# Edge weights of attention and convolution as two 128-row products over 448 columns instead of four 64-row products over 224

## The reference, cut to what matters

```
x = _layernorm(x + L0(x, edge_attr_16, edge_attr_4, ...))   # attention over edges
x = _layernorm(x + L1(x, edge_attr_64, edge_attr_4, ...))   # convolution over edges

L0:  w1 = rbf @ W_rbf                 # rbf (E,16), W_rbf (16,224): five sets of edge weights
     m1_s, m1_v = _cg_tp(msg_s, msg_v, y0, y1, w1[:, :64], w1[:, 64:128],
                         w1[:, 128:160], w1[:, 160:192], w1[:, 192:224])
L1:  w  = edge_query @ tp_weight      # edge_query (E,64), tp_weight (64,224)
     # the same five kinds of products of node features, edge directions and w,
     # then a sum over the edges of each target node
```

## Time and profile before

| | us |
|---|---|
| median of 3 runs | 7921.6 |
| lowest and highest | 7917.41, 7922.39 |
| the profiled execution, its own time | 7914.6 |
| its span | 7912.8 |

### The profile page before, as it was taken

The page is one execution under the profiler, slowest core; times in us unless marked ns, Lnnn a source line. Parts: engine busy times, 40 slices in busy tenths (PEclk is TensorE's granted clock), DMA queues, the critical chain, the costliest instruction groups (busy, mean ns, idle before and its releaser), DMA issues. The chain is left out here.

```text
span 7912.8 us, 199441 instructions
## 1 busy us (share of the span) xinstructions
PE 7045.1 (89%) x48227; PEld 5905.9 (75%) x48227; DVE 7568.2 (96%) x18615; ACT 5259.2 (66%) x18286; POOL 5348.1 (68%) x5500
## 2 busy tenths in 40 slices
PE   6999999999999999999999859998888888888888
PEld 4888888888888888888888848875555555555556
DVE  4999999999999999999999889976999999999999
ACT  2666666666666666666666634435788788788786
POOL 2777777777777777777777436634777777777773
PEclk5999999999999999999999979977999999999999
DMA  3444444434434344343434337732333333333332
GB/s 105 107 109 109 106 107 106 107 106 106 107 105 107 106 107 106 106 108 105 107 106 107 89 128 260 257 117 69 94 93 91 90 91 90 91 91 90 91 91 59
DMA packets 815660, 856.41 MB, mean 108 GB/s; under 512 B 413920, under 2 KB 623200, under 8 KB 815072
## 3 DMA queue, kind: packets, MB, share of 16 engines
q0 software_dynamic: 241920, 413.20, 21.8%
q1 hardware_dynamic: 573088, 438.30, 18.1%
q10 hardware_dynamic: 576, 4.01, 0.1%
HBM read 706.51 MB, written 148.44 MB: 108 GB/s over the span
## 5 line engine op out<-in xcount | busy, mean ns | idle before, releaser
L1243 POOL DMA_INDIRECT agg<-tab_conv,ce_idx x1808 | 1708.7, 945 | 841.3 <-issue 621.8
L471 POOL DMA_INDIRECT ae_gdst<-tab_dst,ae_idx x1616 | 1683.9, 1042 | 528.0 <-issue 528.0
L468 POOL DMA_INDIRECT ae_gsrc<-tab_src,ae_idx x1616 | 1538.5, 952 | 674.4 <-issue 523.9
L1333 PE MATMUL psum<-ce_prod,ce_plain 128*128 128x384 f32 x3616 | 1539.7, 507 | 302.5 <-ACT ce_prod L1318 302.1
L1318 ACT ACTIVATE ce_prod<-ce_raw,ce_y 128x64 f32<-128x64 f32 x5424 | 1464.8, 333 | 0.0
L1316 ACT ACTIVATE ce_prod<-ce_raw,ce_y 128x160 f32<-128x160 f32 x1808 | 753.2, 417 | 488.8 <-DVE ce_raw L1264 488.8
L1335 PEld LDWEIGHTS psum<-ce_prod,ce_plain 128*128 128x128 f32 x3616 | 687.6, 190 | 479.6 <-issue 1.5
L713 ACT ACTIVATE ae_second_t<-psum 128x512 f32<-128x512 f32 x1212 | 732.2, 604 | 462.0 <-PE psum L623 456.1
L1333 PEld LDWEIGHTS psum<-ce_prod,ce_plain 128*128 128x128 f32 x3616 | 546.9, 191 | 449.5 <-DVE ce_plain L1294 276.2
L631 PE MATMUL psum<-pack_sb,ae_first_t 128*128 128x200 f32 x3232 | 850.1, 345 | 2.2 <-ACT ae_first_t L709 2.0
L641 PE MATMUL psum<-pack_sb,ae_second_t 128*128 128x96 f32 x3232 | 665.1, 288 | 129.1 <-ACT ae_second_t L713 126.7
(11 more groups left out here) (216 smaller groups left out, 19066.1 us busy)
## 6 DMA issues: line engine op xcount, KB each, us to landing
ag_val<-h_dram SPq DMA_DIRECT2D x452, 320.0 KB, 4.0
h_dram<-ae_hout SPq DMA_DIRECT2D x404, 320.0 KB
agg<-in_query SPq DMA_DIRECT2D x452, 128.0 KB
ae_rin<-in_rin SPq DMA_DIRECT2D x404, 128.0 KB
agg<-tab_conv,ce_idx POOLq DMA_INDIRECT x1808
ae_gsrc<-tab_src,ae_idx POOLq DMA_INDIRECT x1616
ae_gdst<-tab_dst,ae_idx POOLq DMA_INDIRECT x1616
ce_idx<-in_eidx SPq DMA_DIRECT2D x452, 4.0 KB
```

Source lines behind the costliest of these rows:

```text
L468: pool.indirect_dma_start(gsrc[t.slot4][:, k, :], None, g["tab_src"], bass.IndirectOffsetOnAxis(ap=idx[t.slot4][:, k:k + 1], axis=0))\
L471: pool.indirect_dma_start(gdst[t.slot4][:, k, :], None, g["tab_dst"], bass.IndirectOffsetOnAxis(ap=idx[t.slot4][:, 4 + k:5 + k], axis=0))\
L1243: pool.indirect_dma_start(node[t.slot8][:, k, :], None, g["tab_conv"], bass.IndirectOffsetOnAxis(ap=idx[t.slot8][:, k:k + 1], axis=0))\
L1333: pe.matmul(b_a[t.slot], plain[t.slot4][:, k, :], prod[t.slot][:, k, 96:480], start=(k == 0), stop=False, skip_group_check=True)
```

## The change

The edge weights of both stages are made by two products over all 128 rows, each with 448 moving columns (224 for each of two edge tiles), one PSUM bank to a product. The weight matrices are laid out as blocks with zeros beside them so that the tiles stay apart: `wy` gets 4 x 224 columns, `tp` 448. The query values are laid out on the host so that rows 0 to 63 hold tile 0 (or 2) and rows 64 to 127 tile 1 (or 3). Three more constants are scaled at line 316, and a small tile of the softmax stage (`rows`) is placed in memory that `agg` leaves free there.

```diff
-    ("iota", 128, 128), ("wy", 128, 2 * WY), ...
+    ("iota", 128, 128), ("wy", 128, 4 * WY), ...
-    ("ts1", 64, 128), ("tv1", 96, 192), ("tp", 128, 224),
+    ("ts1", 64, 128), ("tv1", 96, 192), ("tp", 128, 448),
@@ attention_input
-                            for lo, hi, const in ((128, 160, 2 ** -0.5), (160, 192, 0.5), (192, 224, 3 ** -0.5)):
+                            for lo, hi, const in ((128, 160, 2 ** -0.5), (160, 192, 0.5), (192, 224, 3 ** -0.5),
+                                                  (352, 384, 2 ** -0.5), (384, 416, 0.5), (416, 448, 3 ** -0.5)):
@@ attention_edges, TensorE
-                        for k in (0, 2, 1, 3):
-                            q, half = slice(64 * (k // 2), 64 * (k // 2) + 64), WY * (k % 2)
-                            ins = pe.matmul(b_w[:, k, :], rbfy[t.slot][q, :], w("wy")[q, half:half + WY], start=True, stop=True)
+                        for k in (0, 2):
+                            ins = pe.matmul(b_w[:, k:k + 2, :], rbfy[t.slot][:, :], w("wy")[:, WY * k:WY * k + 2 * WY]
+                                            .rearrange("p (k c) -> p k c", k=2), start=True, stop=True)
@@ segment_softmax
-        rows = sb("rows", [H, 2, 2, P])
+        rows = g["agg"][0:H, :, :].rearrange("p b c -> p (b c)")[:, 0:4 * P].rearrange("p (d a q) -> p d a q", d=2, a=2)
@@ conv_edges, TensorE
-                        for k in (0, 2, 1, 3):
-                            q, e = CS * (k // 2), P * (k % 2)
-                            ins = pe.matmul(b_w[t.slot][:, k, :], query[t.slot8][q:q + CS, e:e + P], w("tp")[q:q + CS, :],
-                                            start=True, stop=True)
+                        for e in range(2):
+                            ins = pe.matmul(b_w[t.slot][:, 2 * e:2 * e + 2, :], query[t.slot8][:, P * e:P * e + P],
+                                            w("tp").rearrange("p (k c) -> p k c", k=2), start=True, stop=True)
@@ lay_pack, lay_inputs (host)
-    for lo in (0, 32, 64, 96):
-        own = W["wy"][lo:lo + 32, WY * (lo // 32 % 2):]
+    for k in range(4):
+        own = W["wy"][32 * k:32 * k + 32, WY * k:WY * k + WY]
-    W["tp"][0:64], W["tp"][64:128] = tp, tp
+    W["tp"][0:64, 0:224], W["tp"][64:128, 224:448] = tp, tp
-    query = np.pad(...).reshape(SUPER, 2, 256, 64)
-    query = query.transpose(0, 1, 3, 2).reshape(SUPER, P, 256)
+    query = np.pad(...).reshape(SUPER, 2, 2, P, 64)
+    query = query.transpose(0, 2, 4, 1, 3).reshape(SUPER, P, 256)
```

More of the change, by code:

```diff
@@ L49 @@
     ("ones", 128, 128), ("count", 128, STEPS), ("sidx", 128, 4),
-    ("iota", 128, 128), ("wy", 128, 2 * WY), ("m1_0", 128, 200), ("m1_1", 128, 96), ("m1_2", 96, 96), ("val_t", 64, 128),
+    ("iota", 128, 128), ("wy", 128, 4 * WY), ("m1_0", 128, 200), ("m1_1", 128, 96), ("m1_2", 96, 96), ("val_t", 64, 128),
     ("wg", 64, 32), ("adot", 128, 72), ("m2_0", 128, 96), ("m2_1", 128, 96), ("m2_2", 128, 96),
@@ L1545, in lay_inputs @@
     right = np.concatenate([y0, np.ones_like(rbf)], 2).reshape(SUPER, P, P)
-    query = np.pad(np.asarray(i["edge_attr_64"]), ((0, E - EDGES), (0, 0))).reshape(SUPER, 2, 256, 64)
-    query = query.transpose(0, 1, 3, 2).reshape(SUPER, P, 256)
+    query = np.pad(np.asarray(i["edge_attr_64"]), ((0, E - EDGES), (0, 0))).reshape(SUPER, 2, 2, P, 64)
+    query = query.transpose(0, 2, 4, 1, 3).reshape(SUPER, P, 256)
     return dict(
```

## The result

| | before | after |
|---|---|---|
| median | 7919.51 us (4 runs, 7913.49 to 7922.39) | 7997.74 us (4 runs, 7994.76 to 8002.87) |
| ratio | | 1.0102, 95% interval 1.0087 to 1.0117 |
| profiled execution, its span | 7914.6, 7912.8 us | 8002.87, 8000.5 us |

The change makes the kernel 78 us slower; 8010 was predicted, in a range of 7955 to 8085.

What follows compares the result with a forecast made beforehand. VectorE was taken to set the pace of both stages. 7914.6 us profiled + 88 (convolution) + 0 (attention) + 0.3 = 8003, plus 7 for the median: 8010; own range 8001 to 8046, widened to 7955 to 8085.

Steps and rivals of the forecast that it cites:

- The block of products: Convolution's L1345 on TensorE: four 128-row records one behind another last 1.72 us instead of 1.03, ending 0.57 later.
- the switch from 128 to 64 rows: Between L1335's sums and L1345: a 0.12 us gap put down to it, expected to go with the change.
- the two halves of the rows: L1345's 64-row products in different halves run side by side, four pairs streaming 0.78 us against 1.56 for the new products.
- The slack: Convolution, between the products' end and VectorE's L1261: 0.18 us of cover over two steps.
- The step: Convolution: each step goes to 5.49 us, 0.195 more, adding 88 us over 452 steps.
- The total: Whole kernel: 8003 us for the profiled execution, 8010 us for the median of the runs.
- Attention: Attention's edge stage: products 0.60 us longer, hidden in TensorE's 0.71 us free, 0.11 left; cost 0.
- Rival (2): Attention too becomes bound by TensorE, the block growing over 0.71 us: about 8034 us, or 8094 with upper bounds; chance 0.10.
- (1): Cost hidden: products end less than 0.18 us later or TensorE makes up the time; 7922 us; chance 0.11.
- (3): All-row weight loads on TensorE are exposed once per record, in convolution and attention: 8300 us; chance 0.02.
- (4): Faster, by half the instructions and a gain at each switch of row halves: about 7915 us; chance 0.03.
- The rest: Three more scalings at L316 cost 0.3 us; larger constants, query layout and the softmax tile's place cost nothing.

Runs made afterwards that it cites:

- the order 0, 1, 2, 3: Kernel before with convolution's four 64-row products ordered 0, 1, 2, 3 instead of 0, 2, 1, 3: ratio 1.0046 on a chip at 11574.12 us.
- two doses: Kernel before with one or two more pairs of 64-row products ahead of convolution's four: 7954.47 and 8041.20 us, against 7917.56.
- one pair more: Kernel before with one added pair of 64-row, 224-column products ahead of convolution's four: 7954.47 us, ratio 1.0046.
- attention alone: Kernel before with only attention's edge weights made by two 128-row products: ratio 0.9898, 11473.82 against 11592.96 us.
- the turn of products and sums: TensorE's convolution products of step m+1 put ahead of the sums of step m-1: kernel before 0.9929; changed kernel 0.9745, 0.9744, 0.9741 against kernel before.

## Why the prediction was right

The mechanism was right where the time is decided: products that end later behind the sums, a small cover over two steps, the rest recurring in convolution, nothing in attention. The sizes were near, and in the total some errors cancelled.

**The block of products.** Forecast 1.72 us, measured 1.70. It was forecast to begin 0.12 us sooner behind the sums, as the switch from 128 to 64 rows goes. The last record of the sums, L1336 (L1335 before), shows it in the kernel after:

```profile
6503.94 0.36 PE L1336 MATMUL psum<-ce_prod,ce_plain 128*128 128x96 f32 x2
```

From there to L1345 at 6504.14 are 0.20 us; before it was 6512.27 to 6512.56, 0.29. So about 0.10 came back where 0.12 was forecast, the block grew by 0.67 where 0.69 was, and the end moved by 0.57, as forecast.

**Why they ran two at a time.** The prediction had the products in the two halves of the rows run side by side. The pairs are in its rows; the halves as their cause failed their test, since the order 0, 1, 2, 3 pairs as well. The forecast time doesn't hang on it, as it needs only that 64-row products pair and 128-row ones don't.

**The slack.** Forecast 0.18 us per two steps from a single pair of steps; two doses and the changed kernel give 0.20 to 0.21. That one pair was so near the mean was luck, as the cover of single pairs of steps goes from 0.10 to 0.27 in the kernels with one pair more and with the change.

**The step.** Forecast 5.49 us in the middle of the stage, measured 10.96/2 = 5.48. Forecast +88 us, measured +82 in the stage; the 6 between them are the slack (0.205 instead of 0.18: 0.025/2 x 452 = 6 us). The forecast had VectorE wait 0.2 us in every step; it waits in every second one, 0.27 us in the mean over the stage (58.7 us in 216 waits). These idle times come to less than the 82 us because VectorE's records overlap when nothing is waited for: L1262 at 6511.18 begins 0.08 us before the record of the instruction ahead of it ends, so a delay of 0.46 shows as 0.38.

**The total.** The sum of 8003 us for a profiled execution met 8002.87, partly by luck: the stage took 6 less than forecast, and 4 ahead of it and 1.4 behind it were no part of the sum. The 7 us added for the median went the wrong way, as the median lies 5 under the profiled execution: 7997.74 against 8010. It lies 3 us below the forecast's own range of 8001 to 8046; what holds it is the widening to 7955 for the slack, the very term that was too small.

**Attention.** Forecast hidden with 0.11 us left; 0.13 left. The growth from L681 to L624 was forecast as 0.60 and is 0.63. Rival (2), attention bound by TensorE, is out, but by an eighth of a microsecond.

**Rivals (1), (3) and (4).** The products end 0.57, not under 0.18 us later; weight loads of all 128 rows aren't exposed, since twice as many of them leave the block as it was; and nothing got faster at 7.9 ms, since VectorE sets the pace.

**The rest**, 0.3 us, is below what can be seen.

## What to carry to other kernels

An engine's idle share says nothing of what a longer instruction costs: look at which side of the idle time it stands. Follow the chain from its reader back to itself, count the steps that it spans, and take the difference to that many steps as the cover. Beyond it a delay cost its length divided by the steps, at all three lengths tried here. Read the cover from several steps, as single ones differ. Products over 64 rows ran two at a time here, so that filling them up with zeros to 128 rows made the block 1.70 us long instead of 1.03, for the same results. And where a longer block can't be avoided, try another place for it among the engine's instructions: ahead of the sums the same block left the steps at 5.30 us.

## What the runs showed of the hardware that wasn't expected

**64-row products pair in either order**: 1.03 us for eight records with the order 0, 2, 1, 3 and with 0, 1, 2, 3.

**The length of VectorE's records.** L1261 has a mean of 759 ns in the earlier trace rows and 686 ns in the changed kernel, with nothing of the instruction changed. It isn't the change that does it: the kernel before has both lengths in one execution (679 to 806 ns over its 452 records), and the kernel before with one more pair has, in its groups by shape of the same 1000 us,

```profile
L1261 DVE TENSOR_TENSOR ce_raw<-psum,agg 128x512 f32<-128x512 f32 x186 | 127.7, 687 | 7.7 <-PE psum L1348 4.4
```

and attention alone, with convolution as before, has records of 0.69 us too (below). The pace of VectorE is the same with either (5.30 us a step where nothing is waited for), so such a record holds time that the next instruction doesn't wait for.

**Chips on which the same program takes 11.6 ms.** The windows of attention alone there, in the middle of attention and of convolution, in the columns of the earlier trace rows:

```profile
1000.00:2000.00 1000.00, 738.49 (x4408) 656.45 (x4408) 622.50 (x1625) 428.20 (x1276) 458.05 (x464) 0.82 0.25 66
9000.00:10000.00 1000.00, 738.96 (x3386) 497.69 (x3385) 757.43 (x1697) 600.50 (x2262) 534.01 (x564) 0.89 0.29 68
```

No engine is full, and TensorE's granted clock, 1.00 in the earlier trace rows, is 0.82 and 0.89 in the mean. The timeline of one step of convolution there shows what a standstill looks like:

```profile
8996.70 1.03 PE L1345 MATMUL psum<-pack_sb,agg 64*128 64x224 f32 x8
...
8998.28 0.28 DVE L1306 TENSOR_TENSOR ce_prod<-psum,ce_dot 128x128 f32<-128x128 f32 x1
...
9001.47 0.69 DVE L1261 TENSOR_TENSOR ce_raw<-psum,agg 128x512 f32<-128x512 f32 x1 [2.91 <-remote]
```

The products end at 8997.73, VectorE's instruction ahead at 8998.56, and L1261 begins 2.91 us later with no releaser that the profile knows. Between two such standstills the steps take 5.30 us as elsewhere. There the change doesn't cost: attention's part makes the kernel 1% faster, convolution's 0 to 0.4%, and the turn of products and sums 0.7% in the kernel before; all three together make 2.6%, where at 7.9 ms the change costs 1%. (The change as it is, without the turn, wasn't timed there; with four products instead of two it came to 0.9897.) The changed kernels have fewer instructions on TensorE, and the turned ones make their products earlier; that either is the reason wasn't tried, nor what the chips differ in.
